# Second attention: the weighted sum reads 9 value columns per head from a packed tile, in place of 32 padded with zeros

## The reference

```
x: (2, 256, 128)   ctx: (2, 512, 128)   16 heads of 8
q = heads(layernorm(x) @ W_Q + b_Q)
k = heads(ctx @ W_K + b_K)
v = heads(ctx @ W_V + b_V)
weights = softmax(q k^T / sqrt(8))          # per batch and head, 256 x 512
out = weights @ v                           # per batch and head, 256 x 8
x = x + tanh(g_xattn[1]) * (combined(out) @ W_O + b_O)
```

## Time and profile before

| | |
|---|---|
| runs, us | 187.03, 184.26, 185.22 |
| median, us | 185.22 |
| profiled execution, us | 183.6 |
| its span from the first to the last instruction, us | 181.8 |
| mean granted TensorE clock, as a share of 2.4 GHz | 0.981 |

### The profile page before, as it was taken

The page is one execution under the profiler, slowest core; times in us unless marked ns, Lnnn a source line. Parts: engine busy times, 40 slices in busy tenths (PEclk is TensorE's granted clock), DMA queues, the critical chain, the costliest instruction groups (busy, mean ns, idle before and its releaser), DMA issues.

```text
span 181.8 us, 3378 instructions
## 1 busy us (share of the span) xinstructions
PE 155.2 (85%) x1245; PEld 104.9 (58%) x1250; DVE 109.9 (60%) x296; ACT 85.8 (47%) x148; POOL 64.0 (35%) x95
## 2 busy tenths in 40 slices
PE   0599995798999998987979999989876866799994
PEld 0257873744599875744434444436435634499994
DVE  1579777796734377999977888862415795001032
ACT  2133726432084017569777787788710456201020
POOL 6489924896392521699300000000204541000000
PEclk9999999699999999999999999999999799999999
DMA  6999900015787670012510000000023000000002
GB/s 161 393 336 422 392 26 2 0 45 130 173 177 168 187 285 0 4 43 45 70 20 0 0 0 4 0 0 4 0 78 157 0 2 2 4 0 0 4 0 65
DMA packets 4294, 15.43 MB, mean 85 GB/s; under 512 B 948, under 2 KB 1844, under 8 KB 3492
## 3 DMA queue, kind: packets, MB, share of 16 engines
q1 hardware_dynamic: 2980, 11.66, 20.5%
q10 hardware_dynamic: 576, 2.44, 4.0%
q0 software_dynamic: 720, 1.09, 2.9%
HBM read 13.94 MB, written 1.25 MB: 84 GB/s over the span
## 4 chain that ended last, share of the span: by engine, by line
PE 63%; DVE 14%; POOL 8%; issue 6%; DMA 5%; ACT 3%; POOLq 0%; ACTq 0%
PE bank L483 58%; PE bank L487 5%; DMA fc1T_sb<-q_rows 3%; POOL fc1T_sb L462 2%; POOL q_rows L457 2%; DVE top L1250 2%; DVE k L1252 2%; DMA x_sb<-in_x 2%; DVE stats L1168 2%; POOL rstd L372 1%; POOL xb L391 1%; DVE normed L1173 1%; DVE meanvar L1169 1%; DVE res_b L1224 1%; DVE mx L1363 1%
## 5 line engine op out<-in xcount | busy, mean ns | idle before, releaser
L1363 DVE TENSOR_REDUCE mx<-bank 128x1 f32<-128x512 f32 x64 | 41.9, 688 | 6.4 <-PE bank L483 6.0
L1098 ACT ACTIVATE arena<-bank 128x1024 f32<-128x1024 f32 x32 | 32.1, 1025 | 9.4 <-PE bank L483 8.9
L483 PE MATMUL bank<-kpack,fc1T_sb 72*128 72x512 bf16 x64 | 22.7, 383 | 1.7 <-DMA fc1T_sb<-q_rows 1.0
L368 POOL TENSOR_SCALAR rstd<-meanvar 128x2 f32<-128x2 f32 x10 | 2.2, 223 | 60.9 <-DVE meanvar L1169 60.9
L483 PE MATMUL bank<-fc1T_sb,kpack 104*128 104x256 bf16 x128 | 19.3, 272 | 0.1
L483 PE MATMUL bank<-arena,va 128*32 128x256 f32 x256 | 18.6, 387 | 0.5 <-ACT outT L1092 0.5
L483 PEld LDWEIGHTS bank<-fc1T_sb,kpack 104*128 104x128 bf16 x128 | 12.0, 97 | 6.2 <-issue 1.6
L483 PEld LDWEIGHTS bank<-kpack,fc1T_sb 72*128 72x128 bf16 x64 | 6.1, 97 | 12.2 <-issue 5.4
L487 PE MATMUL bank<-const_sb,normed 128*128 128x128 f32 x16 | 4.3, 339 | 9.6 <-DVE normed L1173 9.6
L483 PE MATMUL bank<-selq_bf,zeros_bf 128*128 128x512 bf16 (+1 forms) x44 | 10.2, 372 | 2.0 <-issue 1.8
L483 PE MATMUL bank<-normedT,shGU_sb 128*128 128x256 f32 (+1 forms) x24 | 9.3, 533 | 1.4 <-issue 1.4
(11 more groups left out here) (231 smaller groups left out, 310.6 us busy)
## 6 DMA issues: line engine op xcount, KB each, us to landing
kpack<-k_parts SPq DMA_DIRECT2D x3, 768.0 KB
fc1T_sb<-in_fc1T SPq DMA_DIRECT2D x1, 2048.0 KB, 12.2
fc_sb<-in_fc SPq DMA_DIRECT2D x1, 2048.0 KB, 16.5
fc_sb<-in_gateup ACTq DMA_DIRECT2D x2, 1024.0 KB, 6.5
arena<-in_down SPq DMA_DIRECT2D x1, 1024.0 KB, 4.8
k_parts<-arena SPq DMA_DIRECT2D x8, 96.0 KB, 2.2
fc1T_sb<-q_rows POOLq DMA_DIRECT2D x9, 64.0 KB, 2.9
ctxT_sb<-in_ctxT SPq DMA_DIRECT2D x2, 256.0 KB, 4.6
```

The source lines that it names most:

```text
L368: pool.tensor_scalar(rstd[:, k, i:i + 2].unsqueeze(2), meanvar[:, k, i:i + 2, 1:2], EPS, None, ALU.add)\
L483: return pe.matmul(o, lhsT, rhs, start=start, stop=stop, **k)
L1098: act.activation(probs1[:, n % (2 * GH), :, :], bank[:, 2 + 2 * (n % 2):4 + 2 * (n % 2), :], ACT.Exp, scale=SCALE)\
L1363: dve.tensor_reduce(mx1[:, b * 2 + qt, g * GH + j:g * GH + j + 1], bank[:, r, :], AX_X, ALU.max)\
```

## The change

The tile `va1` becomes a view `[128, 8, 16, 9]` of the first 1152 columns of a flat tile of 3328: 8 values and the 1, heads side by side, with no zeros. The memset of 4096 columns goes, the memset of the ones stays, with a step of 9 columns in place of 32. The ACT copies write with the same step. Each matmul of `weighted` takes 9 columns as its stationary operand, and writes 9 partitions from 0, 32, 64 or 96. In the built program each still has a tile of 128 rows by 32 columns at the same positions of the array. The other 23 partitions of each 32 in bank 6 keep what earlier matmuls left there; they are still copied and turned, and nobody reads them. The semaphore `va1_zero` is `va1_ones` now, and counts to 1. All later tiles of the attention begin 3072 bytes lower in each partition; the views of `va1_flat` keep their places in it.

```
-        va1 = sb("va1", [P, NB * KC, H, 32])
+        va1_flat = sb("va1_flat", [P, 3328])[:]
+        va1 = va1_flat[:, 0:NB * KC * H * (DH + 1)].rearrange("p (c h w) -> p c h w", c=NB * KC, h=H)
...
-        va1_flat = va1[:].rearrange("p c h w -> p (c h w)")
...
             pool.wait_ge(S["k0_sb"], 1)
-            pool.memset(va1[:], 0.0).then_inc(S["va1_zero"], 1)
-            pool.wait_ge(S["va1_zero"], 1)
-            pool.memset(va1[:, :, :, DH:DH + 1], 1.0).then_inc(S["va1_zero"], 1)
-            pool.wait_ge(S["va1_zero"], 2)
+            pool.memset(va1[:, :, :, DH:DH + 1], 1.0).then_inc(S["va1_ones"], 1)
+            pool.wait_ge(S["va1_ones"], 1)
             pool.memset(late[ZROW:P, :], 0.0).then_inc(S["kpack_zero"], 1)
...
                 for j in range(GH):
-                    ins = mm(bank[32 * j:32 * j + 32, 6, 0:SQ], va1[:, b * KC + kc, g * GH + j, :],
+                    ins = mm(bank[32 * j:32 * j + DH + 1, 6, 0:SQ], va1[:, b * KC + kc, g * GH + j, :],
                              probs1[:, (u % 2) * GH + j, kc, :], start=kc == 0, stop=kc == KC - 1)
...
-            act.wait_ge(S["va1_zero"], 2)
+            act.wait_ge(S["va1_ones"], 1)
             for c in range(NB * KC):
                 act.wait_ge(S["v1_ps"], KC * (c // KC + 1))
                 act.copy(va1[:, c, :, 0:DH], bank[:, 2 + c // KC, (c % KC) * P:(c % KC + 1) * P]
```

More of the change, by code:

```diff
@@ L291, in build @@
             "yT_ps", "yT_sb", "kept_ps", "kept_sb", "b2w_sb", "fc1_ps", "hid_sb", "hidg_sb", "fc2_ps", "moe0_sb",
-            "sc_ps", "xg_sb", "k1_ps", "v1_ps", "bias1_ps", "k1_sb", "k1_hi", "k1_rest", "k1_mid", "va1_zero", "va1_sb", "bias1_sb", "k3_sb",
+            "sc_ps", "xg_sb", "k1_ps", "v1_ps", "bias1_ps", "k1_sb", "k1_hi", "k1_rest", "k1_mid", "va1_ones", "va1_sb", "bias1_sb", "k3_sb",
             "kpack_in", "nT2_ps", "nT2_sb", "q1_ps", "q1_sb", "q3_sb", "ring_full",
```

## The result

The changed kernel is slower. Four runs each: 187.26 us median (186.21 to 187.79) against 185.75 (184.26 to 187.03), a ratio of 1.0133 with a 95% interval from 1.0086 to 1.0179. (Some executions of any kernel fall in a slower state; the ratios compare the fast ones alone, so they are not quotients of the medians.) A second set beside other kernels gave 1.0149 (1.0101 to 1.0196). So it costs about 1.4%, 2.5 to 2.8 us, where 0.3 us less was forecast, and the time lies outside the stated range. By the bound of 2% it still reads as the same. The profiled execution took 187.14 us with a span of 185.3, 3.5 us over that of before.

A forecast was written before the change was run, and what follows sets the result against it. PE's queue was taken to bound the kernel from 93.4 to about 134 us, in the second attention. 14 groups at 21 ns gave 0.29 us, all other terms nothing: 185.22 - 0.3 = 184.9 us, range 183.1 to 187.0 us.

The forecast's parts named there:

- the stated range: Range forecast for the time: 183.1 us, which is 183.6 less 0.5, to the slowest run of before, 187.0.
- The weight loads and the groups that count: Weighted sum: exposed first-round loads fall from 109 to about 88 ns; 14 groups at 21 ns save 0.29 us.
- The group in ACT's shadow: One of three groups per full unit, as at 103.66 us: its saving only lengthens `raw_scores`' wait on ACT.
- lost concurrency: Rival, weighted sum: four heads no longer run side by side; about 221 us, or 197 with two; 3 in 100.
- slow loads: Rival, weighted sum: loads at 36-byte steps make first rounds 20 ns slower, 0.28 us in all, 185.5 us; 10 in 100.
- The memset on POOL: Start of the kernel: 3.51 us at 9.92 us go, `kpack`'s memset, bias and `xb` move up; worth nothing.
- the prediction's own signs of being wrong: A round not 0.215 us, 93.36 us to attention's end moving over 0.5 us, or anything before 50 us following POOL.
- `xb` would be done near 19.8 us: POOL's `xb`, done at 23.32 us before, moves up; slack to DVE's read grows from 1.5 to 5 us.
- The clock: Rival, 1.2 GHz stretch after the attention: gone, 1.4 us more gain, 183.5 us; doubled, 186.3 us; 10 in 100 together.

The follow-up runs named there:

- Experiment 2: Kernel before, 32 columns, with only the order of three GpSimd memsets changed, `kpack`'s first: 1.0111 (1.0068 to 1.0154) of the kernel before.
- 1: Changed kernel with one memset of about 2.9 us put back on GpSimd ahead of the ones: 0.9998 (0.9964 to 1.0032) of the kernel before.
- 5: Changed kernel with `kpack`'s memset waiting for DVE's two `bvcol` copies, run twice: 0.9969 (0.9931 to 1.0007) and 0.9983 (0.9946 to 1.0021) of before.
- 3: Changed kernel with the two `bvcol` copies written as `tensor_tensor` maximum, GpSimd untouched: 0.9984 (0.9950 to 1.0018) of the kernel before.
- 4: Kernel before, 32 columns and both memsets, with the two `bvcol` copies written as `tensor_tensor` maximum: 1.0006 (0.9966 to 1.0045) of before.
- 8: Changed kernel measured again with no further edit, beside other kernels: 1.0149 (1.0101 to 1.0196) of the kernel before.
- 9: Changed kernel, `kpack`'s memset behind the `bvcol` copies, 22 filler matmuls for 28, `atleast` reading PSUM: 0.9940 (0.9909 to 0.9971) of before.
- experiment 6: Changed kernel with `kpack`'s memset cut into four pieces of 2048 columns, without waits between: 1.0013 (0.9973 to 1.0053) of the kernel before.
- 7: Changed kernel with `bvcol` copies as `tensor_tensor`, 22 filler matmuls for 28, `atleast` reading PSUM: 0.9966 (0.9927 to 1.0005) of the kernel before.

## Why the prediction was wrong

*The weight loads and the groups that count: right.* The load of 9 columns was put at 88 ns and is 89; 14 groups times 21 ns was 0.29 us, and the path from the landing to the last group is 0.27 us shorter. The group in ACT's shadow gave its saving to the wait, as forecast. The rivals of lost concurrency and of slow loads are out: eight more matmuls still cost 0.43 us (0.98 - 0.55), so a round is 0.215 us as before with 9 partitions written, and the loads got shorter. The rule that the prediction quotes from the Trainium skill, page "TensorE: Matmul & The Clock Gate", section "LDWEIGHTS (loading the stationary operand)", gave 19 ns a load by its slope, and the rows show 20; its total, columns divided by 1.2, leaves out some 80 ns that every load has here.

*The memset on POOL: wrong, and the whole miss.* The prediction said of it: "Ends: nothing on both sides, since no one waits for either." I looked for who waits on GpSimd's semaphores, and priced what moves up as harmless because it is early. The one that is hurt waits on no semaphore: DVE's `tensor_copy` from SBUF to SBUF is held while a GpSimd memset runs. Experiment 2 shows it without the layout, 1 and 5 undo it in two ways with the layout in place, 3 undoes it from DVE's side. The term that was missing is + 3.71 us at DVE's first maximum, of which 3.1 to 3.4 us reach the search for top scores in the traces set side by side above. One of the prediction's own signs of being wrong came true: something before 50 us follows POOL. Its forecast that `xb` would be done near 19.8 us failed too: it is done at 22.04 (20.34 + 1.70), since `gbias` waits for a bias that PE makes from `bvcol`.

*Why the runs lost less than the pair of traces.* Executions start differently. From DVE's first `k` instruction (L1189 before) to the second, which waits for PE, it is 1.7 to 1.8 us in three traces (before, and both of experiment 5) and 2.9 in four (3, 4, 8, 9), where PE's early matmuls take longer (last section). From that first `k` to the first `MAX8`, with no copy held, it is 24.5 to 24.6 us in the quick three, and 25.9 to 26.2 in 3, 4 and 9. With the copies held behind the whole memset it is 27.6 to 28.0 in all three traces (changed, 2, 8), though these three started differently. So the hold costs 3.0 to 3.5 us against a quick start and 1.4 to 2.1 against a slow one, where PE is late in any case: its value projection starts at 17.36 us in experiment 4, against 15.87 in the kernel before and 18.17 in the changed one. The runs' 2.5 to 2.8 us lie between. How often an execution starts one way or the other was not counted, so this account of the size is argued, not shown.

*It could have been read.* The trace of before had the row: two copies of 128 by 128 in 2.01 us, ending with GpSimd's memset, where another copy of the same size from SBUF to SBUF (L1184) takes

```profile
7.72 0.28 DVE L1184 COPY va<-const_sb 128x128 f32<-128x128 f32 x1
```

Each of the two takes 1.9 us, seven times its like: a wait that isn't in the column of idle times. Had it been read so, moving the 6.92 us memset from 13.90 to 10.4 would have put DVE's copies, ready at 11.6 us, behind 10.4 + 6.9 = 17.3 us: 3.8 us, to be set against the slack of PE's path.

The Trainium skill states it on the page "SBUF — State Buffer", section "SBUF: two separate sides": VectorE and GpSimd share a pair of ports under an exclusive lock, whoever starts first has it for the whole instruction, and VectorE needs it in its two-port modes, or with two inputs in SBUF against a GpSimd instruction that reads SBUF. The traces agree on each part that they touch: the copies wait for the whole instruction (17.2 us) and no longer than the piece that runs (14.2 us in experiment 6), and two SBUF inputs pass a memset, which reads nothing (0.48 us for two in experiment 3). That the copies run in a two-port mode is not shown by any run here. This rule spoke against the change, and the prediction did not weigh it.

*The clock.* It was a rival with 1.4 us either way, and it moved, without deciding. The profiled execution of before had 1.2 GHz for two stretches of 3.4 us; the changed one for 6.8 us near 35 to 42 us, and none after the attention:

```profile
37.00:42.00 5.00, 5.00 (x21) 3.96 (x21) 4.63 (x16) 2.81 (x11) 4.47 (x4) 0.52 0.00 2
142.00:147.00 5.00, 2.51 (x28) 2.09 (x29) 2.45 (x11) 1.92 (x4) 2.01 (x5) 1.00 0.00 0
```

The kernel before's second window has 0.66 there. The missing stretch after the attention saved nothing. From the last group of value matmuls to the end of the span it is 49.08 us before (181.8 - 132.72), 49.02 in the changed kernel (185.3 - 136.28), and 49.04 in experiment 8, which has the stretch; in experiments 1 and 9, where it lasts 6.8 us, it is 49.4 and 48.9. So the prediction's 1.4 us for it doesn't hold: PE is busy there, but losing the stretch didn't bring the end nearer. The longer stretch ahead does cost something. `above` (L1260), DVE's first instruction behind PE's filler matmuls and the transposes of the grade, waits 0.99 to 1.36 us for PE in the six traces with a stretch of 6.8 us and 28 filler matmuls (changed, 1, 2, 3, 4, 6), and 0.38 or 0.39 in the four with 3.4 us (before, both of 5, 8). The changed kernel and experiment 8 are the same program. Their searches start 0.23 us apart, `above` 0.97 and batch 1's queries 0.62 (97.19 against 96.57). Between these two the longer stretch costs about 0.4 us, and as much of it is in the loss of the first pair of profiles, which shows 3.5 us where the runs show 2.5 to 2.8. It is why the stretches between two fixed events were compared, and the medians of many runs, and not two spans.

*What stays open.* Why experiment 2 lost 2.0 us and the changed kernel about 2.6 with nearly the same delay at the first maximum (16.82 and 17.21 us): `kpack`'s memset starts 0.4 us later in the changed kernel, but its layout gives 0.27 us back, so most of the difference is unexplained; the intervals overlap. The step in experiments 7 and 9 has two edits, the shorter filler and the comparison, and how they share the gain was not tried. Their traces show both at work: `atleast` is shorter, and `above` waits 0.39 us for PE though the lower clock lasts 6.8 us.

## What to carry to other kernels

When an instruction is taken out of GpSimd's queue, ask not only who waits for its semaphores but which VectorE instructions will now run beside what moves up: here SBUF-to-SBUF copies were held until a running memset was over, and a comparison with one SBUF input until a subtraction was. A VectorE row that takes several times what its like takes elsewhere may be such a wait, and it has no entry in the idle time. Put long memsets behind such copies with a wait, cut them up, or give the VectorE instruction a form that isn't held; work that looks like idle filler may be what keeps the two apart.

## What the runs showed of the hardware

- A held VectorE instruction is drawn as busy: its row starts when it could have started and lasts until it is done (4962 ns for a copy that takes 219 ns when nothing runs on GpSimd).
- GpSimd seems to be held by VectorE too. In experiment 6 the third piece of the memset, which meets the end of the copies, takes 1946 ns, and the three others 1800. That is one row, and no run tests it.
- A float32 weight load takes 89 ns for 9 columns, 109 for 32, 137 for 64: 0.9 ns a column on top of some 80. It is worth something only where it is exposed, in the first round of a group.
- A matmul with 9 columns of its 32-column tile in use runs beside its three neighbours as one with 32 does; the streaming time does not change.
- At the start of the program TensorE's matmuls take about twice their later time, as at the lower of its two clocks, though the row of granted clock says 1.00 there. In the kernel before, two matmuls of 512 float32 columns take 1.92 us at 7.08 us, and four take 1.88 at 10.70. How long this lasts varies between executions: the matmul of 512 columns at 9.84 us in the kernel before took 595 ns, the same one at 9.98 us in the changed kernel 1061. It moved DVE's second `k` instruction against the first by up to 1.2 us between single profiles (1.71 to 2.91), and the search for top scores by as much as 1.7 (24.5 to 26.2 from the first `k`), over half of the effect that was looked for.
